# The last chunk of the mixture stage finished in two halves, a quarter of a wide sum moved on TensorE, and a fill instead of an addition behind each gather

## What is computed

```
x = layernorm(x + wave_attention(x))
x = layernorm(x + fp4_ffn(x))
x = layernorm(x + window_attention(x))
x = layernorm(x + experts(x) + shared(x))
```

```
scores = softmax(x @ Wr)                       # 8 experts
w, idx = top_k(scores, 2);  w = w / sum(w)
y_e    = (silu(x @ Wg[e]) * (x @ Wu[e])) @ Wd[e]   # only the two chosen experts count
out    = w[0] * y_idx[0] + w[1] * y_idx[1]
out   += (silu(x @ Sg) * (x @ Su)) @ Sd        # the shared expert, all tokens
```

## Time and profile before

| | before |
|---|---|
| median of three runs | 1142.85 us (1139.61 to 1143.18) |
| the profiled execution's own time | 1140.53 us |
| its span in the trace | 1138.5 us |
| mean granted TensorE clock | 0.965 |
| busy: TensorE, VectorE, ScalarE, GpSimd | 91%, 70%, 40%, 41% |
| start of tile 0's transposes | 645.9 us |
| last expert tile's result copied | 1018.3 us |
| last `down_s` of TensorE ends | 1127.0 us |
| last normalised strip | 1134.1 us |

### The profile page before, as it was taken

The page is one execution under the profiler, slowest core; times in us unless marked ns, Lnnn a source line. Parts: engine busy times, 40 slices in busy tenths (PEclk is TensorE's granted clock), DMA queues, the critical chain, the costliest instruction groups (busy, mean ns, idle before and its releaser), DMA issues.

```text
span 1138.5 us, 19200 instructions
## 1 busy us (share of the span) xinstructions
PE 1030.8 (91%) x5944; PEld 900.1 (79%) x5945; DVE 792.5 (70%) x1339; ACT 460.0 (40%) x781; POOL 465.3 (41%) x451
## 2 busy tenths in 40 slices
PE   4879974659999999999999999998999999999993
PEld 3657753659999999899997788887888888888883
DVE  7978989699999998678878634343444443447876
ACT  6835434334444444466763122222232232233326
POOL 3211013224555444522210388785751300018884
PEclk9989987689999999999999999999999999999997
DMA  7100020000000000031142256656333111213335
GB/s 290 38 19 19 0 84 0 33 1 1 1 0 0 0 0 2 1 122 51 38 142 100 80 171 185 221 172 197 110 106 106 55 51 51 74 56 109 114 102 184
DMA packets 41204, 87.80 MB, mean 77 GB/s; under 512 B 5954, under 2 KB 27716, under 8 KB 39748
## 3 DMA queue, kind: packets, MB, share of 16 engines
q0 software_dynamic: 9696, 35.66, 10.2%
q1 hardware_dynamic: 20660, 39.20, 9.6%
q10 hardware_dynamic: 10800, 12.32, 3.5%
HBM read 57.80 MB, written 29.36 MB: 77 GB/s over the span
## 4 chain that ended last, share of the span: by engine, by line
PE 55%; DVE 15%; DVEq 10%; issue 8%; POOL 8%; ACT 2%; POOLq 1%; DMA 1%; another core or an unknown queue 1%; ACTq 0%
PE PS L1724 15%; PE PS L1726 14%; PE PS L1725 14%; POOL gathered L990 5%; PE PS L2096 3%; PE PS L1848 3%; DVEq L1312 2%; DVEq L1208 2%; POOL pause L994 1%; DVEq L1324 1%; DVE hx L1220 1%; PE PS L2080 1%; PE PS L1753 1%; DVEq L1221 1%; DVE qinv L1211 1%
## 5 line engine op out<-in xcount | busy, mean ns | idle before, releaser
L1665 DVE TENSOR_TENSOR hb<-PS,gs 128x512 f32<-128x512 f32 x71 | 49.1, 692 | 153.0 <-ACT gs L723 137.0
L990 POOL DMA_INDIRECT gathered<-expert_outputs,pos x64 | 66.5, 1039 | 139.1 <-DMA expert_outputs<-ye 126.8
L1724 PE MATMUL PS<-EWs,xeh 128*128 x284 | 119.3, 420 | 1.6 <-DVE xel L1659 1.6
L1726 PE MATMUL PS<-EWs,xel 128*128 x284 | 111.9, 394 | 0.0
L1725 PE MATMUL PS<-EWs,xeh 128*128 x284 | 111.6, 393 | 0.0
L723 ACT ACTIVATE gs<-PS 128x512 f32<-128x512 f32 x71 | 42.5, 599 | 160.9 <-PE PS L1726 143.5
L1724 PE MATMUL PS<-WGh,bxh 128*128 128x352 f32 x256 | 88.5, 346 | 14.1 <-DVE hv L1306 12.1
L1848 PE MATMUL PS<-WD,htf 128*128 128x256 f32 x384 | 88.5, 380 | 1.6 <-ACT htf L519 1.5
L1724 PE MATMUL PS<-EWs,heh 128*128 x284 | 85.6, 301 | 0.9 <-issue 0.9
L1725 PE MATMUL PS<-WGl,bxh 128*128 128x352 f32 x256 | 85.8, 335 | 0.0
L1726 PE MATMUL PS<-WGh,bxl 128*128 128x352 f32 x256 | 85.6, 334 | 0.0
(11 more groups left out here) (363 smaller groups left out, 3078.7 us busy)
## 6 DMA issues: line engine op xcount, KB each, us to landing
raw_of<-experts POOLq DMA_DIRECT2D x6, 1536.0 KB
expert_outputs<-ye SPq DMA_DIRECT2D x71, 128.0 KB
xe<-tokens_by_expert ACTq DMA_DIRECT2D x65, 128.0 KB
xraw<-xT SPq DMA_DIRECT2D x8, 512.0 KB, 5.3
X<-x SPq DMA_DIRECT2D x1, 4096.0 KB, 16.8
tokens<-X SPq DMA_DIRECT2D x8, 512.0 KB, 3.3
y<-X SPq DMA_DIRECT2D x8, 512.0 KB
raw_of<-experts SPq DMA_DIRECT2D x2, 1536.0 KB, 9.0
```

What stands on the lines that cost most here:

```text
L990: pool.indirect_dma_start(out=gathered[c][:, j, t], out_offset=None, in_=YS, in_offset=bass.IndirectOffsetOnAxis(ap=pos[:, j, 4 * c + t:4 ...
L1665: dve.tensor_tensor(hb[:, h], PS[:, 3], gs[:, h], ALU.mult).then_inc(e_hb, 1)
L1724: pe.matmul(out_, wh, vh, start=first, stop=False)
L1726: return pe.matmul(out_, wl, vh, start=False, stop=last_)
```

## The change

**The quarter.** On TensorE three quarters of `down_wide(1)` are done, then the transposes of expert tile 0, then the fourth quarter.

**The pause.** Behind each gather of chunks 0 to 5 GpSimd fills the 28 elements with zeros instead of adding zeros to zeros.

**The last chunk.** The gathers of chunk 7 count on two semaphores, one for strips 0 and 1 and one for strips 2 and 3. VectorE, after step 3 of `shared(7)`, finishes strips 0 and 1 (gated, added, statistics), then strips 2 and 3. GpSimd computes the deviations of each half by itself, and its waits for `d_mv` stand outside `deviation4`. ScalarE normalises strips 0 and 1 and then strip 2, VectorE strip 3. SyncE stores the two halves separately, nine stores in all.

**What moves with it.** ScalarE normalises chunk 0 behind step 2 of `shared(7)` and chunk 1 behind step 3, and chunks 2 to 6 after that. VectorE does the statistics of chunk 6 behind step 3 instead of step 2.

```diff
@@ sync
             for c in range(NCH):
                 sp.wait_ge(d_ln, c + 1)
-                if c == NCH - 1:
-                    sp.wait_ge(d_last, 1)
-                sp.dma_start(out[:, bass.ds(4 * c, 4)], X[:, bass.ds(4 * c, 4)]).then_inc(s_out, 16)
-            sp.wait_ge(s_out, 16 * NCH)
+                strips = 4 if c < NCH - 1 else 2
+                sp.dma_start(out[:, bass.ds(4 * c, strips)], X[:, bass.ds(4 * c, strips)]).then_inc(s_out, 16)
+            sp.wait_ge(d_last, 1)
+            sp.wait_ge(d_ln_last, 1)
+            sp.dma_start(out[:, bass.ds(4 * NCH - 2, 2)], X[:, bass.ds(4 * NCH - 2, 2)]).then_inc(s_out, 16)
+            sp.wait_ge(s_out, 16 * (NCH + 1))
@@ scalar
-                if end == 4 or c == NCH - 1:
-                    last_.then_inc(d_ln, 1)
+                last_.then_inc(d_ln, 1)
...
-            shared(7, chunks=(((0, 0, 4),), ((1, 0, 4),), ((2, 0, 4),), ()))
-            for c in range(3, 6):
+            shared(7, chunks=((), (), ((0, 0, 4),), ((1, 0, 4),)))
+            for c in range(2, NCH - 1):
                 normalise(c, 0, 4)
-            normalise(6, 0, 4)
             normalise(NCH - 1, 0, 2)
+            act.wait_ge(d_rs_last, 1)
+            at = 4 * (NCH - 1) + 2
+            act.activation(X[:, at], X[:, at], ACT.Identity, scale=rstd4[:, NCH - 1, 2:3], bias=nmr4[:, NCH - 1, 2:3]).then_inc(d_ln_last, 1)
@@ gpsimd
-                                                ).then_inc(d_gr[c], 16)
+                                                ).then_inc(d_gr_last if c == NCH - 1 and t >= 2 else d_gr[c], 16)
                         if c < 6:
-                            pool.tensor_tensor(pause[:, 4 * c + t, j], zrow[:, 0:28], zrow[:, 0:28], ALU.add)
+                            pool.memset(pause[:, 4 * c + t, j], 0.0)
...
+            pool.wait_ge(d_mv, 4)
             deviation4(0, 0, 4)
             gather(NCH - 1)
+            pool.wait_ge(d_mv, 6)
             deviation4(1, 4, 6)
+            pool.wait_ge(d_mv, 7)
             deviation4(2, 6, 7)
-            deviation4(3, 7, 8)
+            pool.wait_ge(d_mv, 8)
+            deviation4(3, 7, 8, slice(0, 2))
+            pool.wait_ge(d_mv_last, 1)
+            deviation4(4, 7, 8, slice(2, 4), d_rs_last)
@@ vector
-            shared(7, (((), (5, 3)), ((6, 0), (6, 1)), ((6, 2), (6, 3)), ()), ((5,), (), (6,), ()))
-            for part in range(4):
-                gated(NCH - 1, part)
-            added(NCH - 1)
-            statistics(NCH - 1)
-            dve.wait_ge(d_rs, NCH)
-            for i in range(2, 4):
-                at = 4 * (NCH - 1) + i
-                last_ = dve.tensor_scalar(X[:, at], X[:, at], rstd4[:, NCH - 1, i:i + 1], nmr4[:, NCH - 1, i:i + 1], ALU.mult, ALU.add)
-            last_.then_inc(d_last, 1)
+            shared(7, (((), (5, 3)), ((6, 0), (6, 1)), ((6, 2), (6, 3)), ()), ((5,), (), (), (6,)))
+            last = NCH - 1
+            gated(last, 0)
+            gated(last, 2)
+            added(last, (0,))
+            statistics(last, range(0, 2))
+            dve.wait_ge(d_gr_last, 16 * 4)
+            gated(last, 1)
+            gated(last, 3)
+            added(last, (1,))
+            statistics(last, range(2, 4), d_mv_last)
+            dve.wait_ge(d_rs_last, 1)
+            at = 4 * last + 3
+            dve.tensor_scalar(X[:, at], X[:, at], rstd4[:, last, 3:4], nmr4[:, last, 3:4], ALU.mult, ALU.add).then_inc(d_last, 1)
@@ tensor
-            down_wide(1)
+            down_wide(1, 0, 3)
             x_transpose_e(0, 0)
+            down_wide(1, 3)
```

More of the change, by code:

```diff
@@ L991, in gather, with deviation4 @@
                                                 in_offset=bass.IndirectOffsetOnAxis(ap=pos[:, j, 4 * c + t:4 * c + t + 1], axis=0)
-                                                ).then_inc(d_gr[c], 16)
+                                                ).then_inc(d_gr_last if c == NCH - 1 and t >= 2 else d_gr[c], 16)
                         if c < 6:
-                            pool.tensor_tensor(pause[:, 4 * c + t, j], zrow[:, 0:28], zrow[:, 0:28], ALU.add)
[L996 to L1002, removed]
+                            pool.memset(pause[:, 4 * c + t, j], 0.0)
+            def deviation4(n, first, end, strips=slice(0, 4), done=d_rs):
+                chunks, width = slice(first, end), strips.stop - strips.start
+                eps, half = (C[:, at:at + width].unsqueeze(1).to_broadcast([P, end - first, width]) for at in (C_EPS, C_HALF))
+                zeros = zrow[:, 0:width].unsqueeze(1).to_broadcast([P, end - first, width])
+                pool.tensor_tensor(rstd4[:, chunks, strips], mv4[:, chunks, strips, 1], eps, ALU.add)
+                pool.tensor_tensor(nmr4[:, chunks, strips], zeros, mv4[:, chunks, strips, 0], ALU.subtract).then_inc(p_dev, 1)
                 pool.wait_ge(p_dev, 2 * n + 1)
-                pool.tensor_tensor(rstd4[:, chunks], rstd4[:, chunks], half, ALU.pow).then_inc(p_dev, 1)
+                pool.tensor_tensor(rstd4[:, chunks, strips], rstd4[:, chunks, strips], half, ALU.pow).then_inc(p_dev, 1)
                 pool.wait_ge(p_dev, 2 * n + 2)
-                pool.tensor_tensor(nmr4[:, chunks], nmr4[:, chunks], rstd4[:, chunks], ALU.mult).then_inc(d_rs, end - first)
+                pool.tensor_tensor(nmr4[:, chunks, strips], nmr4[:, chunks, strips], rstd4[:, chunks, strips], ALU.mult).then_inc(done, end - first)
             pool.wait_ge(e_st0, 16 * ((NE + 1) // 2))
@@ L1590, in _, with added @@
                               ALU.mult).then_inc(d_tile, 1)
-            def added(c):
+            def added(c, halves_=(0, 1)):
                 if c >= AHEAD:
                     dve.drain()
-                for w in range(2):
+                for w in halves_:
                     dve.wait_ge(d_dn, 2 * c + w + 1 if c < AHEAD else down_parts(c, 3) + w - 1)
@@ L1625, in gated, with statistics @@
                     dve.scalar_tensor_tensor(X[:, at], gathered[c][:, part // 2, t], gate[:, part // 2, at:at + 1], X[:, at], ALU.mult, ALU.add)
-            def statistics(c):
+            def statistics(c, strips=range(4), done=d_mv):
                 h = c % 2 * 4
                 dve.drain()
-                for i in range(4):
+                for i in strips:
                     dve.bn_stats(st6[:, h + i], X[:, 4 * c + i])
                 dve.drain()
-                for i in range(4):
+                for i in strips:
                     last_ = dve.bn_aggr(mv4[:, c, i], st6[:, h + i])
-                last_.then_inc(d_mv, 1)
+                last_.then_inc(done, 1)
             def shared(c, parts=((), (), (), ()), done=((), (), (), ())):
@@ L2037, in token_table, with down_wide @@
                 mm.then_inc(d_table, 1)
-            def down_wide(c):
+            def down_wide(c, first=0, end=4):
                 bank = BANK[c]
                 pe.wait_ge(d_ld, 32)
-                for j in range(4):
+                for j in range(first, end):
                     pe.wait_ge(d_hb, 4 * c + j + 1)
```

3 lines of the change are left out of this document (2 added, 1 removed).

## The result

| | before | after |
|---|---|---|
| median of four runs | 1141.51 us (1139.61 to 1143.18) | 1189.62 us (1188.05 to 1192.30) |
| ratio, 95% interval | | 1.0423 [1.0409, 1.0437] |
| profiled execution, span | 1140.53, 1138.5 us | 1188.82, 1186.7 us |
| mean granted TensorE clock | 0.965 | 0.943 |

The forecast was 1135.9 us, faster; the change made the kernel 48 us slower. As the experiments show, the whole loss is the fill's. It is there in the runs of the result and on two chips of the experiments, and absent on a third, where the changed kernel takes 0.9938 of the time of before. So the result has two halves: a stall that was not foreseen, and under it the gain that was.

The account below looks back on a forecast made before the run. TensorE was taken to bound most of the kernel, with a chain of small steps after the gathers. The end's 4.35 us and the quarter's 1.25 made 5.6 off 1141.5, giving 1135.9 us, range 1132.3 to 1140.2.

Parts of the forecast that it names:

- the pause: Behind gathers of chunks 0 to 5: shorter fills bring gathers at least 4.7 us earlier, ending VectorE's 2.13 us wait; worth 1.4.
- 1.4 worse: Rival that the fill is no shorter, so VectorE still waits for chunk 4: 1137.3 us, chance 0.15.
- Slower: Rival: unexplained hitches in the expert loops, 5 us each; two more give 1146 us, chance 0.05; one more, 0.05.
- The larger sum: Thirty-nine pauses before the fortieth gather: 8.2 us saved if VectorE's disturbances go, against 4.7 if they stay.
- The normalising moved: In shared(7): hb of step 1 comes 4.15 us earlier, and from there to Hl takes 9.8 us, another 1.2 less.
- The halves: Last chunk: VectorE's path 11.9 us after Hl; ScalarE's 26 strips take 12.9 us, finishing 13.4 after Hl and ending the writing.
- the fill's part of the tail: Earlier gathers end VectorE's wait for chunk 4's rows; worth 0.99 to 2.13 us, taken as 1.4.
- The quarter: Before expert tile 0: a quarter of down_wide(1) fills TensorE's 1.18 us idle; products start 1.25 us earlier, bounds 0 to 1.5.
- the second rival: The quarter fails because rows land late or expert-loop pauses use up the lead: 1137.2 us, chance 0.15.
- The sum: Whole kernel: 4.35 us at the end plus 1.25 from the quarter, 5.6 us off 1141.5, giving 1135.9 us.
- the tail: End of the kernel: ScalarE's last strip 4.1 us earlier, GpSimd's last deviation 4.5 earlier; taken as 4.35 us without the quarter.

Follow-up runs that it names:

- add_of_four: The changed kernel with an addition over four elements as the pause instead of the fill of 28; 1137.96 us, ratio 0.9963 on chip A.
- halves_alone: The kernel before with the last chunk in halves, the normalising moved and an addition over four elements as the pause, quarter not moved; 1130.80 us, ratio 0.9967.
- change_again: The changed kernel, unedited, run again on chip D beside the kernel before; 1127.63 us, ratio 0.9938.
- halves_quarter_add: The changed kernel with the addition over 28 elements put back as the pause, halves and quarter kept; 1138.61 us, ratio 0.9980 on chip A.
- quarter_alone: The kernel before with the moved quarter of down_wide(1) alone; 1141.32 us, ratio 0.9999 on chip B.

## Why the prediction was wrong, by its steps

**The step that failed** is the pause. The prediction costed the fill by its length and by who waits for the gathers: "I take at least 4.7, so the wait goes", "More than 2.1 us buys nothing there". That held: 0.14 us each (forecast 0.12), no DMA wait left. It treated a pause that nobody reads as time on GpSimd's queue and nothing else. What it missed is that the pause also spaces the gathers, and that on some chips closer gathers all but stop the other three engines. The upper side of this step's range was "1.4 worse"; the fill by itself cost 47.1 us on chip A (1188.76 - 1141.68). A purpose for an instruction without a reader should have been asked for, and the trace had the sign: the rival "Slower" named exactly these unexplained waits of ScalarE and said that nothing explained them. It had the right symptom, but placed it in the expert loops, at 5 us each and 0.05, as luck of the instruction string, and did not connect it to GpSimd's fetches, which run beside those tiles. That the two are of one kind is likely, not shown for each wait. Pausing the fetches took 5 us more off on a chip of that kind (0.9916 against 0.9963 for add_of_four; the two are from different chips), and nothing on chip D (0.9963, as halves_alone on C).

**The Trainium skill on the fill.** "SBUF — State Buffer", Who interferes with whom: a VectorE instruction with two inputs from SBUF gets in the way of a GpSimd instruction that reads SBUF, not of one that only writes it. The trace agrees (121 to 158 ns against 239 to 1131). The larger sum, 8.2 us of earlier gathers, was the better one: from the first gather to the fortieth it is 51.9 us in change_again where it was 60.8 before, 8.8 less. What was right for GpSimd's queue is also what brought the gathers so close.

**The normalising moved: right.** In change_again VectorE and ScalarE from step 1 of `shared(7)`; VectorE's rows answer to the earlier trace rows:

```profile
1098.03 0.66 DVE L1650 TENSOR_TENSOR hb<-PS,gs 128x512 f32<-128x512 f32 x1
...
1102.59 0.68 DVE L1650 TENSOR_TENSOR hb<-PS,gs 128x512 f32<-128x512 f32 x1
...
1107.81 0.69 DVE L1655 TENSOR_TENSOR Hl<-hb,Hh 128x512 fp32r<-128x512 f32 x1 [0.69 <-ACT Hh L708]
...
1119.68 0.41 DVE L1730 TENSOR_SCALAR X<-X,rstd,nmr 128x256 f32<-128x256 f32 x1 [1.51 <-POOL nmr L1009]
```

`hb` of step 1 follows on the statistics of chunk 5 with no wait (4.15 before), and from it to the last `Hl` it is 9.78 us, forecast 9.8.

**The halves: right.** VectorE's last strip starts 1119.68 - 1107.81 = 11.9 us after `Hl`, forecast 11.9. ScalarE's rows of the same run answer to the earlier trace rows:

```profile
1107.68 12.87 ACT L697 ACTIVATE X<-X,nmr,rstd 128x256 f32<-128x256 f32 x26
1120.46 0.58 ACT L769 ACTIVATE X<-X,nmr,rstd 128x256 f32<-128x256 f32 x1
```

26 strips in a row, 12.87 us (forecast 12.9), and the end 1121.04 - 1107.81 = 13.2 after `Hl` (13.4). GpSimd's drain ends the program at 1119.4 + 5.5 = 1124.9, its length kept. From the first gather to the end of the span it is 1125.2 - 1012.6 = 112.6 us where it was 117.8 (first gather at 1020.7): 5.2 us less, forecast 4.35. With additions as the pause (halves_quarter_add, 1137.7 - 1023.2 = 114.5) it was 3.3 less; the fill's part of the tail is then 1.9, forecast 1.4, as far as runs on different chips can be compared.

**The quarter: mechanism right, worth wrong.** The gap of 1.18 us is gone; TensorE in after:

```profile
644.14 0.38 PE L2092 MATMUL PS<-C,xe 128*128 128x128 f32 x2
644.35 1.89 PE L2057 MATMUL PS<-wide_down,inner 128*128 128x256 f32 x8
645.90 0.58 PE L1736 MATMUL PS<-EWs,xeh 128*128 x1
```

The products start 1.59 us earlier than before (647.49), forecast 1.25. But the gathers start at 1020.47 instead of 1020.73: the lead was used up in the expert tiles, and quarter_alone is 0.9999. That is the second rival (0.15).

**The sum.** 5.6 us of 1141.5 is a ratio of 0.9951. Where the fill does no harm (chip D) the changed kernel has 0.9938 [0.9918, 0.9958]: the total was close for what it counted, in part by luck. The measured gain there is 6.6 us (1134.18 - 1127.63). The quarter's 1.25 of the forecast 5.6 are worth nothing that quarter_alone shows on B, and the tail gave 0.85 more than its 4.35.

## What to carry to other kernels

Before a seemingly idle instruction between DMA issues is made shorter, ask what it keeps apart: measure the distance from one issue to the next and look at whether engines that share nothing with those transfers stop at once, with "remote" or "issue" as the only reason. Before a low count is called the cause (here the instruction packets), set it against the work done: a count per matmul showed it to be a result. Idle time that a trace can't explain is to be explained before it is called chance, above all where GpSimd issues indirect DMAs close together; an addition of 0.2 us behind each took 1189 us back to 1138 where the fill stalled, and gained 5 us more behind the token fetches. It isn't free: on chip D, where nothing stalls, the version with additions was 3.6 us slower than the one with the fill of 224 elements. And run a kernel on several chips before believing a gain of half a per cent: the same change was 4.2% slower in one place and 0.6% faster in another.

## What the runs showed that was not expected

- Indirect DMAs of 128 rows issued every 1.26 us can nearly stop TensorE, VectorE and ScalarE for 40 us (one silu: 40.81 us), with the DMA engines only 0.36 busy. Halving the bytes changes nothing (1.0451); additions between them, 1.42 us median and 1.54 mean, cure it. On another chip the same 1.26 us stop nothing.
- Chips differ (or the times at which they ran): the kernel before took 1141 to 1142 us on A, B and in the runs of the result, all of which stalled with the short fill, and 1134 on C, D and E; D, the only one of these that ran the short fill, did not stall.
- Successive small fills on GpSimd start 0.05 us apart, though one lasts 0.14: two are no longer a pause than one.
- In the stall as without it there is one packet of the instruction queue q8 for 127 to 135 matmuls, and ScalarE and TensorE took up work again before any further instruction packet. The stall isn't shown to be one of fetching.
- GpSimd slowed down as well in the end: between 1073 and 1083 us of after its own gathers came up to 2.8 us apart, and only then did ScalarE's silu start, at 1080.55.
